# Cross-attention with an image prompt: one small subtraction moved from VectorE to GpSimd, and two short VectorE operations moved ahead of a reciprocal

## The reference

```python
q = heads(x @ W_q)
probs_t  = softmax(q @ heads(text @ W_k).T * scale)          # 60 text tokens
text_out = probs_t @ heads(text @ W_v)
attn_ip  = q @ heads(ip @ W_k_ip).T * scale                  # 4 prompt tokens
qsem     = l2norm(probs_t @ text)                            # max(norm, 1e-12) guards it
fused    = attn_ip + 0.5 * (qsem @ l2norm(ip).T)
probs_ip = softmax(fused) * spatial_mask
out = (text_out + probs_ip @ heads(ip @ W_v_ip)) @ W_out + b_out + x
```

## Time and profile before

| | |
|---|---|
| runs | 378.09 us median of 3 (377.99 to 379.45) |
| profiled execution | span 376.4 us; only its span is known, no time of its own |
| PE busy | 335.5 us (89%) |
| DVE busy | 325.7 us (87%) |
| ACT busy | 301.9 us (80%) |
| POOL busy | 155.3 us (41%) |
| mean granted TensorE clock | 0.986 |

### The profile page before, as it was taken

The page is one execution under the profiler, slowest core; times in us unless marked ns, Lnnn a source line. Parts: engine busy times, 40 slices in busy tenths (PEclk is TensorE's granted clock), DMA queues, the critical chain, the costliest instruction groups (busy, mean ns, idle before and its releaser), DMA issues.

```text
span 376.4 us, 10174 instructions
## 1 busy us (share of the span) xinstructions
PE 335.5 (89%) x2434; PEld 314.5 (84%) x2434; DVE 325.7 (87%) x2100; ACT 301.9 (80%) x1303; POOL 155.3 (41%) x282
## 2 busy tenths in 40 slices
PE   5899988898989898979899898989898989899965
PEld 4897777787989898979898898979898989899855
DVE  5757379999999999968999999879999999999972
ACT  4646798988989798878898898868898989889940
POOL 2045305555443535444545444333535454423240
PEclk9999999999999999989999999989999999999998
DMA  6940020001010010101010101001010101000000
GB/s 215 331 114 0 14 55 24 2 19 53 21 54 18 20 43 12 57 22 52 19 52 18 53 18 52 21 3 52 19 52 18 53 18 53 18 20 17 21 35 35
DMA packets 14301, 16.72 MB, mean 44 GB/s; under 512 B 1928, under 2 KB 13704, under 8 KB 14248
## 3 DMA queue, kind: packets, MB, share of 16 engines
q1 hardware_dynamic: 14248, 16.20, 14.0%
HBM read 10.13 MB, written 5.24 MB: 41 GB/s over the span
## 4 chain that ended last, share of the span: by engine, by line
PE 61%; DVE 20%; ACT 9%; issue 8%; DMA 1%; SPq 0%; DVEq 0%; ACTq 0%
PE gv_ps L935 15%; PE mi_ps L962 15%; PE mi_ps L898 11%; PE et_ps L922 7%; PE sc_ps L914 6%; ACT e_sb L547 5%; DVE place_ctxT L702 5%; DVE qs L684 2%; DVE negmax L694 2%; ACT qs L539 2%; PE gv_ps L1053 1%; DVE attnT_low L773 1%; DVE attnT_low L776 1%; DVE sip L693 1%; DVE ipd L800 1%
## 5 line engine op out<-in xcount | busy, mean ns | idle before, releaser
L547 ACT ACTIVATE e_sb<-sc_ps,negmax 128x60 f32<-128x60 f32 x640 | 146.3, 314 | 27.2 <-DVE negmax L694 25.0
L935 PE MATMUL gv_ps<-tab,place_w 128*128 128x162 f32 x640 | 115.9, 303 | 2.3 <-ACT place_ctxT L556 2.1
L702 DVE CUSTOM_DVE_ANT_0 place_ctxT<-gv_ps,e_sb 128x60 f32<-128x60 f32 x640 | 100.9, 212 | 9.2 <-PE gv_ps L935 8.5
L935 PEld LDWEIGHTS gv_ps<-tab,place_w 128*128 128x128 f32 x640 | 95.3, 192 | 3.5 <-issue 3.4
L489 POOL TENSOR_TENSOR place_w<-place_ctxT,rsum 128x320 f32<-128x320 f32 x32 | 23.8, 743 | 135.5 <-DVE rsum L812 135.5
L914 PE MATMUL sc_ps<-km,qs 128*128 128x256 f32 x320 | 77.8, 325 | 0.2 <-DVE qs L684 0.2
L922 PE MATMUL et_ps<-ident,e_sb 128*128 128x128 f32 x320 | 64.0, 282 | 11.1 <-ACT e_sb L547 10.5
L694 DVE TENSOR_REDUCE negmax<-sc_ps 128x4 f32<-128x240 f32 x160 | 63.2, 395 | 0.0
L560 ACT COPY place_w<-et_ps 128x256 f32<-128x256 f32 x160 | 62.1, 388 | 1.0 <-PE et_ps L922 1.0
L922 PEld LDWEIGHTS et_ps<-ident,e_sb 128*128 128x128 f32 x320 | 39.1, 140 | 21.4 <-ACT e_sb L547 15.2
L702 DVE DVE_READ_ACCUMULATOR2_ANT quad<- 128x1 f32 x640 | 51.7, 81 | 0.0
(11 more groups left out here) (153 smaller groups left out, 588.9 us busy)
## 6 DMA issues: line engine op xcount, KB each, us to landing
x_nat<-in_x SPq DMA_DIRECT2D x16, 320.0 KB, 3.1
out<-place_w SPq DMA_DIRECT2D x32, 160.0 KB, 1.8
place_ctx<-in_ctx SPq DMA_DIRECT2D x4, 256.0 KB, 3.6
place_w<-in_L_xattn_W_v SPq DMA_DIRECT2D x1, 640.0 KB, 6.8
place_w<-in_L_xattn_W_k SPq DMA_DIRECT2D x1, 640.0 KB, 8.1
place_w<-in_L_xattn_W_k_ip SPq DMA_DIRECT2D x1, 640.0 KB, 9.6
place_w<-in_L_xattn_W_v_ip SPq DMA_DIRECT2D x1, 640.0 KB, 9.6
place_ctxT<-place_w SPq DMA_DIRECT2D x16, 40.0 KB, 1.9
```

Source lines behind the costliest of these rows:

```text
L547: last = nc.scalar.activation(e_sb[:, slot, TOK * j:TOK * j + T], sc_ps[:, bank, TOK * j:TOK * j + T], ACT.Exp, bias=negmax[:, slot, j:j + 1])
L702: last = v.tensor_tensor_reduce(out=junk[:, u % 2, j, 0:T], in0=gv_ps[:, u % 2, TABW * j:TABW * j + T], in1=e_sb[:, u % ERING, TOK * j:TOK ...
L935: last = mm(gv_ps[:, u % 2, 2 * TABW * r:2 * TABW * r + 2 * TABW], eT[:, u % TRING, P * r:P * r + P], tab[:, batch.parity, h:h + 2, :].rea ...
```

## The change

`ipd` is no longer made by DVE in the slot with j = 0. POOL makes it for the same tile at the end of its own list, behind `add_bias` where there is one, as soon as `ipmax` is there. One part of `builds` gets a wait of POOL on its own `ipd`. On DVE, in the slots with j = 2, the order was `iprec`, `rsum`, `guard`, the four products, `quadc`; it becomes `guard`, `iprec`, `quadc`, `rsum`, the four products.

```diff
@@ builds (POOL)
                 if k in (5, 7):
                     pool.wait_ge(fused_made, batch.count(TILES, s))
                     pool.sem_inc(pool_turn, 1)
+                if k == 6:
+                    pool.wait_ge(ipd_made, batch.count(TILES, s - 1))
+                    pool.sem_inc(pool_turn, 1)
@@ tile (POOL)
                 builds(batch, s, 1)
                 if s % 2 == 1 and batch.has(HALVES, s // 2 + 1, ALL_HALVES):
                     add_bias(batch, s // 2 + 1)
+                if batch.has(TILES, s - 1, ALL_TILES):
+                    pool.wait_ge(ipmax_made, n)
+                    g.tensor_tensor(ipd[:, par], fused[:, par], ipmax[:, par].unsqueeze(2).to_broadcast([P, HEADS, NIP]),
+                                    ALU.subtract).then_inc(ipd_made, 1)
@@ slot (DVE)
-                if j == 0 and before2:
-
-                    dve.wait_ge(ipmax_made, n2)
-                    v.tensor_tensor(ipd[:, par2], fused[:, par2], ipmax[:, par2].unsqueeze(2).to_broadcast([P, HEADS, NIP]),
-                                    ALU.subtract).then_inc(ipd_made, 1)
                 if j == 1 and before2:
                     dve.wait_ge(ipe_made, n2)
                     v.tensor_reduce(ipsum[:, par2], ipe[:, par2], AX_X, ALU.add).then_inc(ipsum_made, 1)
+                if j == 2 and before:
+
+                    dve.wait_ge(fin_copied, batch.count(UNITS, GROUPS * s))
+                    ssum = fin[:, par, :, FINW - 1]
+                    v.scalar_tensor_tensor(out=guard[:, par], in0=ssum, scalar=EPS * EPS, in1=ssum,
+                                           op0=ALU.mult, op1=ALU.mult).then_inc(guard_made, 1)
                 if j == 2 and before2:
                     dve.wait_ge(ipsum_made, n2)
                     v.reciprocal(iprec[:, par2], ipsum[:, par2]).then_inc(iprec_made, 1)
                 if j == 2 and before:
-
-                    dve.wait_ge(fin_copied, batch.count(UNITS, GROUPS * s))
-                    ssum = fin[:, par, :, FINW - 1]
+                    dve.wait_ge(guard_made, n)
+                    v.tensor_tensor(quadc[:, par], quad[:, par], guard[:, par], ALU.max).then_inc(quadc_made, 1)
                     v.reciprocal(rsum[:, par], ssum).then_inc(rsum_made, 1)
-                    v.scalar_tensor_tensor(out=guard[:, par], in0=ssum, scalar=EPS * EPS, in1=ssum,
-                                           op0=ALU.mult, op1=ALU.mult).then_inc(guard_made, 1)
...
                 if batch.has(UNITS, u - 1, ALL_UNITS):
                     quadratic(batch, u - 1)
-                if j == 2 and before:
-
-                    dve.wait_ge(guard_made, n)
-                    v.tensor_tensor(quadc[:, par], quad[:, par], guard[:, par], ALU.max).then_inc(quadc_made, 1)
```

## The result

The changed kernel takes 362.97 us (median of 4, 361.83 to 363.88), the kernel before 378.04 beside it: a ratio of 0.9598, interval 0.9561 to 0.9635. The forecast was 365.4 with a range from 363.0, so the direction and the cause were right and the gain was undersized: 15.1 us instead of 12.7, and the time is 0.03 us outside the range. The profiled execution has a span of 361.6 us against 376.4. Measured again on another chip (experiment 8), the same two kernels gave a ratio of 0.9518, and the two intervals do not meet.

A forecast was written before the change was run, and what follows sets the result against it. PE waiting for a nearly full DVE, held by POOL, was the bound. A 6 × 1.0 plus 0.9, B 6.0, together 12.9, less 0.2 in the drain: 12.7; span 363.7, median 365.4 us, range 363 to 371.

The forecast's parts named there:

- The bound, and the hold: PE's output projection waits 16.8 us for DVE's `attnT_low`, late because POOL's bias addition holds `ipd` on DVE.
- Twelve places: Held `ipd`, 1.3 us each: seven at A, five at B; batch 0's A, DVE alone on the chain, gains 0.9.
- Place A, 1.0: Tile 2 of batches 0 to 6: PE's projection starts 1.00 us earlier, PE last or tied with ACT; 1.0 each.
- Place B, 1.2: Tile 0 of batches 1, 2, 4, 6, 7: gain 0.92 to 1.25, at most 1.41; 1.2 us taken each.
- The new order: DVE slots with j = 2: `quadc` falls from 0.35 to 0.175 under PE's work; nothing, at best 5.6 us.
- Turns and tail: At the two loop turns nothing gained; in the drain PE's transposes wait for `pip`, costing 0.2 us.
- POOL's `ipd` at the other places: Other 20 places: DVE saves 0.24 us each under PE's work, POOL's 0.36 is hidden; nothing, bound 4.8 us.
- the later `rsum`: `rsum` comes 0.29 us later, shifting `attn`, `ipw`, `pip` by 0.2 to 0.3; POOL's 0.85 wait for `rnorm` covers it.
- More coming back (2): Short `ipd` and `quadc` savings count as well: 8.6 us beyond the forecast, 357 at the extreme, 361 if half; chance 0.07.
- ACT (1): Start of ACT's exponentials counts, not PE's arrival: 0.50 to 0.83 us a place, 368 to 372 us; chance 0.16.
- The hold did not move to the products (3): Rival claim: the bias addition would hold DVE's products or `attnT_low` instead, leaving 378 us; chance 0.08.
- Slower (4): `ipe` delays the next `exps` and POOL's `ipd` queues behind the bias addition, exponentials come later: 381 us; chance 0.07.

The follow-up runs named there:

- experiment 8: The full change measured once more, unaltered, against the kernel before on another chip: 360.36 us, ratio 0.9518.
- experiment 3: Kernel before with one more wait: POOL's bias addition waits for `ipd`, which stays on DVE; 365.22 us, ratio 0.9643.
- 6: Changed kernel plus a spare DVE subtraction reading two SBUF tensors in the old place of `ipd`, result unread: 375.61 us, ratio 0.9920.
- 7: Changed kernel plus a spare DVE instruction reading one SBUF tensor in the old place of `ipd`, result unread: 362.96 us, ratio 0.9571.
- experiment 4: Changed kernel with POOL making `ipd` ahead of the bias addition instead of behind it: 362.77 us, ratio 0.9588.
- The flat pair: Kernel before and changed kernel, both with the loop written out on PE, ACT, DVE and POOL: 373.59 and 356.55 us.
- the flat kernel: Changed kernel with the loop written out on PE, ACT, DVE and POOL: 356.55 us, ratio 0.9421 against the kernel before.

## Why the prediction was off, point by point

- **The bound, and the hold.** Right. PE waited for DVE at A and B, and DVE was held by POOL. That is shown by taking only the overlap away (experiment 3), and by bringing the hold back with a useless instruction of two inputs, not with one of a single input (6, 7).
- **Twelve places.** Eleven counted. In batch 0 I gave 0.9 us and it gave nothing, although `ipd` stood on the chain there. ACT works without a gap from the exponentials over `ipe` and a part of `u_all` (L650) to the copy that PE's table product waits for. The timeline of the changed kernel (from 65 us) has PE waiting for ACT, as it did before (0.31):

```profile
65.36 0.27 ACT L645 ACTIVATE ipe<-ipd 128x80 f32<-128x80 f32 x1
...
65.54 0.44 ACT L650 CAST u_all<-place_ctxT 80x320 fp32r<-80x320 f32 x1
...
66.25 0.79 PE L936 MATMUL gv_ps<-tab,place_w 128*128 128x162 f32 x4 [0.34 <-ACT place_ctxT L563]
```

  So the path that I had wrong in batch 0 is "DVE alone is the chain": ACT was as late. `ipd` ahead of the bias addition gives nothing there either (experiment 4, 0.05 lost).
- **Place A, 1.0.** Measured 1.12, and 1.06 with only `ipd` moved. PE is last there, as forecast.
- **Place B, 1.2.** Too small: five B give 6.9 and not 6.0. With only `ipd` moved they give 6.3 (1.17 and four times 1.29), and ACT is last there, as I had it. In the change `ipe` starts 0.32 behind the bias addition and `exps` 0.76 behind that, where I had 0.40 and 0.80 to 1.13, and the bias addition itself is 0.29 us earlier against PE. Of that, 0.11 is there with only `ipd` moved; the rest goes with the order.
- **The new order, priced at nothing.** This step failed. I asked only whether the slot with j = 2 is under PE's work, and it is. But the held `quadc` delayed ACT's `rnorm` and with it the POOL chain that ends in the bias addition, behind which POOL's `ipd` queues. Alone it gives 0.2 us a place; on top of `ipd` 0.14 at B and 0.06 at A, 0.9 in all. This is all that the places gave beyond the forecast: with only `ipd` moved A and B give 12.7 together, against 12.9 forecast with batch 0. `quadc` was taken at 0.175 and takes 0.115; `guard` and `rsum` are 0.08 and 0.05 longer than before.
- **Turns and tail, priced at nothing and at a loss of 0.2.** This step failed most: in the profile they give 3.5. Two stretches, the second turn and the drain, ran at 1.2 GHz in the profile before and not in the one after, about 1.5 us each. The flat pair, whose profiles both fell in the drain, differ there by 0.1. The clock is a property of the execution that I profiled, and I had read its low stretches as fixed and gave them no term. For the medians an estimate follows from the rate over the timed runs: from a median clock of 0.986 (the profile before and the later runs of that kernel) to 0.993 it is 0.007, or 1.6 us of the 2.4 beyond the forecast. The order's 0.9 is about the rest. Without the clock the gain would be about 13.5, inside my range; on the chip of experiment 8 the same estimate leaves about 16.
- **POOL's `ipd` at the other places, the later `rsum`.** Nothing of them is seen in the time. POOL's wait before `semn` at the place of the earlier trace rows is 0.49 in the changed kernel instead of 0.85, and still there.
- **Rivals.** More coming back (2) was the nearest, by the order and not by the short `ipd`. ACT (1) was last in batch 0 and by 0.1 to 0.3 at B, and cost little. The hold did not move to the products (3), but `u_all` on DVE, two SBUF inputs, is held to 0.74 to 0.77 us three times in batch 0 (0.49 at most before). Slower (4) is 0.3 us away at A and next to nothing at B.
- **Two sums.** Twelve places at 0.85, less 0.2, are 10.0 and 368.1 us, not 367.5; 0.3 and two waits of 0.25 are 0.8, not 0.75. Neither touches the forecast.

## What to carry to other kernels

When two engines run in parallel and one instruction has two durations, look at what the other engine ran when the long one ended. If it ends 0.1 us behind it each time, take away the overlap first, by a wait on the engine that has time: that was one line and gave 13.2 us where moving the instruction gave 14.4. And price a reordering by the whole loop of waits that starts in the slot, not by the slot's own cover: a held instruction of 0.35 us moved the time of another engine's long instruction some 3 us behind it, and so the end of the hold. When you delay an instruction to see how much it has to spare, read the delay from the trace: three instructions of 0.33 us came to 0.86, and with the planned 1.0 I would have seen room at B where there is none.

## What the runs showed of the hardware that was not expected

- A DVE instruction with two SBUF inputs was held by a POOL instruction that reads and writes SBUF until 0.10 us behind its end, at all twelve places: 0.23 us became up to 1.55. One of the same length with one SBUF input ran beside the same additions in 0.226 to 0.229 us. With DVE first it is POOL that is held: 0.67 us instead of 0.33.
- The same turn of a loop, with PE idle for about 2 us, was followed by the clock at 1.2 GHz in some executions and at 2.4 in others. Two falls that can be compared matmul by matmul cost 1.5 us each; over 99 timed runs 0.01 of mean clock goes with 2.3 us, about 1.1 a fall.
- With the loop written out the changed kernel gains 2.2 and 1.9 us at its two turns against experiment 8, where neither turn fell (3.81 less 1.65, 3.78 less 1.92; the flat kernel's own figures against the kernel before).
